# Packed expert numbers, two waits fewer per tile, and earlier offset reads and result scatters in a mixture-of-experts kernel

## What is computed

```python
x = x + tanh(g_xattn) * xattn(layernorm(x), ctx, ctx)
n = layernorm(x)
logits = n @ Wr + br
idx, gate = argmax(logits), softmax(logits)[argmax]
h = gelu(n @ W1[idx] + b1[idx])          # 128 -> 512
x = x + tanh(g_ffn) * gate * (h @ W2[idx] + b2[idx])
```

## Time and profile before

| | |
|---|---|
| three runs | 315.43, 316.87, 317.26 us; median 316.87 |
| profiled execution | 315.37 us, of which the span is 313.5 |
| mean granted clock of TensorE | 0.924 |
| busy, share of the span | PE 78%, DVE 61%, ACT 53%, POOL 58% |
| the chain that ended last | PE 42%, DVE 13%, nothing shown ("issue") 12%, POOL 10%, ACT 5%, unknown 5% |

### The profile page before, as it was taken

How to read it: one execution, slowest core, us unless ns; L and a number is a source line. 1 busy time by engine, 2 the same in 40 slices (tenths; PEclk the granted TensorE clock), 3 DMA queues, 4 the chain that set the end, 5 groups by cost and what they waited for, 6 DMA issues and landing times.

```text
span 313.5 us, 10518 instructions
## 1 busy us (share of the span) xinstructions
PE 245.5 (78%) x3529; PEld 212.7 (68%) x3529; DVE 191.3 (61%) x638; ACT 166.8 (53%) x481; POOL 182.3 (58%) x222
## 2 busy tenths in 40 slices
PE   1467899988999878889898668697457499999970
PEld 1245778777777756777686547586357499999960
DVE  5548688889898999779977745557023044444420
ACT  2155788877787866787776612526023144444420
POOL 7476557676597974889687630463734045444450
PEclk9997999999999999999999977859759699999995
DMA  7602556364636451525222133012233112100100
GB/s 215 207 17 38 150 140 192 65 171 119 163 89 171 110 137 26 136 47 141 44 43 42 45 79 83 29 41 88 72 92 96 44 34 64 57 28 30 36 19 0
DMA packets 58535, 26.63 MB, mean 85 GB/s; under 512 B 38608, under 2 KB 53989, under 8 KB 58484
## 3 DMA queue, kind: packets, MB, share of 16 engines
q1 hardware_dynamic: 55204, 20.15, 26.2%
q0 software_dynamic: 2272, 4.46, 4.3%
q10 hardware_dynamic: 1008, 1.34, 1.5%
HBM read 16.69 MB, written 5.51 MB: 71 GB/s over the span
## 4 chain that ended last, share of the span: by engine, by line
PE 42%; DVE 13%; issue 12%; POOL 10%; ACT 5%; SPq 5%; another core or an unknown queue 5%; DMA 3%; POOLq 1%; DVEq 0%; ACTq 0%
PE ps L736 12%; PE ps L779 4%; SPq L403 4%; DVE mx L1194 3%; PE ps L720 3%; PE ps L718 3%; PE ps L719 3%; PE ps L794 2%; POOL rot L531 2%; POOL rot_s L533 2%; PE ps L769 2%; PE ps L821 2%; POOL rot L537 2%; PE ps L818 2%
## 5 line engine op out<-in xcount | busy, mean ns | idle before, releaser
L552 POOL DMA_INDIRECT out<-fin,got x39 | 37.9, 972 | 46.2 <-DVE fin L1242 34.9
L504 POOL DMA_INDIRECT rows<-x_all,dest_i x32 | 33.4, 1044 | 29.5 <-DVE x_all L1051 22.3
L1194 DVE TENSOR_REDUCE mx<-ps 128x16 f16<-128x1024 f32 x32 | 39.1, 1221 | 17.3 <-PE ps L794 13.3
L736 PE MATMUL ps<-w_f,hT 128*128 x312 | 48.8, 304 | 0.0
L1242 DVE SCALAR_TENSOR_TENSOR fin<-ps,got 128x128 f32<-128x128 f32 x39 | 13.7, 350 | 55.8 <-PE ps L736 41.3
L736 PEld LDWEIGHTS ps<-w_f,hT 128*128 128x128 f32 x312 | 41.9, 209 | 0.8
L779 PE MATMUL ps<-vx,pr 128*64 128x32 f32 x1024 | 36.9, 226 | 4.4 <-DVE on L1129 2.6
L779 PEld LDWEIGHTS ps<-vx,pr 128*64 128x64 f32 x1024 | 33.5, 141 | 8.3 <-issue 3.1
L649 ACT ACTIVATE hT<-ps 128x512 f32<-128x512 f32 x39 | 23.3, 597 | 29.0 <-PE ps L720 15.5
L581 ACT ACTIVATE pr<-ps 128x1024 f32<-128x1024 f32 x32 | 32.7, 1023 | 10.9 <-PE ps L821 10.6
L821 PE MATMUL ps<-qT,kbd 128*128 128x64 f16 x512 | 35.3, 198 | 2.0 <-issue 2.0
(11 more groups left out here) (155 smaller groups left out, 607.8 us busy)
## 6 DMA issues: line engine op xcount, KB each, us to landing
kbd<-kT SPq DMA_DIRECT2D x128, 32.0 KB
got<-rows SPq DMA_DIRECT2D x39, 72.0 KB, 1.9
w_f<-in_W_rows SPq DMA_DIRECT2D x8, 256.0 KB, 3.0
w_r<-in_W_last_row SPq DMA_DIRECT2D x8, 256.0 KB, 3.4
w_f<-in_L_ffn_W SPq DMA_DIRECT2D x8, 256.0 KB
x_all<-in_x SPq DMA_DIRECT2D x3, 512.0 KB, 4.6
xt_all<-in_x_t SPq DMA_DIRECT2D x3, 512.0 KB, 4.5
ct_all<-in_ctx SPq DMA_DIRECT2D x3, 512.0 KB, 4.5
```

The lines of the kernel that those rows point to most:

```text
L504: pool.indirect_dma_start(out=rows, out_offset=bass.IndirectOffsetOnAxis(ap=dest_i[:, t:t + 1], axis=0), in_=x_all[:, t, :], in_offset=Non ...
L552: pool.indirect_dma_start(out=out_d, out_offset=bass.IndirectOffsetOnAxis(ap=got_i[:, u % GOT, R_ID:R_ID + 1], axis=0), in_=fin[:, u % FRI ...
L736: mm = pe.matmul(o, hT[:, par, c, :], w2_f[:, bass.ds(e, 1), c, :].rearrange("p o n -> p (o n)"), start=False, stop=(c == FC - 1))
L1194: dve.tensor_reduce(mx[:, t % 2, 0:H], ps_s[:, :].rearrange("p (h k) -> p h k", k=S), AX.X, ALU.max).then_inc(mx_done, 1)
```

## The change

1. The expert numbers are packed: a word holds eight of them as digits of three bits. DVE multiplies the comparisons with powers of 8 (`C_OCT`, te_q) and sums seven times eight of them into a word (te_w). The first part has 2 words, the second 4. te_c is padded to a whole number of words and filled with zeros at step 8. PE loads the words and takes a number out of its word by a shift and a mask, once per sorted tile in the code.
2. PE's wait for `f_lo` ahead of the transpose is left out from tile 6 on, and the wait for `f_gelu` ahead of the first layer altogether.
3. SP's first offset load of each part stands ahead of its waits for `g_sent` and `g_fill`.
4. `out_step`: the results of tiles 0, 1 and 2 are scattered at steps 39, 39 and 40, between the row scatters of steps 38 and 41; the others, from step 43 on, one in each step.

```diff
--- before.py
+++ after.py
@@ -43,11 +43,13 @@
 SPLIT = GROUPS[EARLY][1]
 N1 = math.ceil((SPLIT * P - NE * (P - 1)) / P)
 N2 = NS - N1
+PACK = 8
+W1N, W2N = math.ceil(N1 / PACK), math.ceil(N2 / PACK)
 F0 = SPLIT + 14
 STEPS = F0 + NS + 3
 FRING = 20
 
-C_ID, C_COS, C_SIN, C_IOTA, C_REV, C_POW, C_EPS, NCF = 0, 128, 136, 144, 184, 192, 193, 194
+C_ID, C_COS, C_SIN, C_IOTA, C_REV, C_POW, C_EPS, C_OCT, NCF = 0, 128, 136, 144, 184, 192, 193, 194, 202
 K_ID, K_TRI, K_ONE, K_EXP, K_SEL, K_BASE, NCH = 0, 128, 256, 384, 1408, 2432, 2440
 
 
@@ -69,6 +71,7 @@
     f[:, C_REV:C_REV + NE] = NE - np.arange(NE)[None, :]
     f[:, C_POW] = -0.5
     f[:, C_EPS] = EPS
+    f[:, C_OCT:C_OCT + PACK] = 8.0 ** np.arange(PACK)[None, :]
     h[:, K_ID:K_ID + P] = np.eye(P)
     h[:, K_TRI:K_TRI + P] = r[:, None] < r[None, :]
     h[:, K_ONE:K_ONE + P] = 1
@@ -207,10 +210,10 @@
         done = sb("done", [P, NE])
         room = sb("room", [P, NE - 1])
         jump = sb("jump", [P, 2, NE - 1])
-        te_c = sb("te_c", [1, NS, NE - 1])
+        te_c = sb("te_c", [1, (W1N + W2N) * PACK, NE - 1])
+        te_q = sb("te_q", [1, W1N + W2N, PACK, NE - 1])
         off_c = sb("off_c", [1, NS, NE - 1])
-        te_f = sb("te_f", [1, NS])
-        te_i = sb("te_i", [1, NS], I32)
+        te_w = sb("te_w", [1, W1N + W2N], I32)
         first = sb("first", [1, NS])
         off_f = sb("off_f", [1, 2, NS])
         off_i = sb("off_i", [1, NS], I32)
@@ -326,7 +329,7 @@
             return 16 * sum(1 for v in range(NS) if pair(v) % ring == pair(u) % ring and pair(v) <= pair(u))
 
         def out_step(u):
-            return max(F0 + 3 + u, max(SCATTER_AT) + 1 + u // 2)
+            return F0 + 5 + u // 2 if u < 3 else min(max(SCATTER_AT) - 2 + u, STEPS - 1)
 
         def used(which, u):
 
@@ -436,21 +439,25 @@
                     alone(sp, sp_passed)
                 sp.dma_start(got[:, slot, :], rows[bass.ds(offset, P), :]).then_inc(f_got[pair(t) % (GOT // 2)], 16)
 
-            def row_tiles(a, b):
+            def offsets(t, b):
+
+                return nc.values_load_multi_w_load_instructions(
+                    off_i[0:1, t:min(t + 8, b)], engines=[SP_ENGINE], min_val=0, max_val=SORTED - P,
+                    skip_runtime_bounds_check_because="a tile starts in the region of its expert or on the last blank rows")[1]
+
+            def row_tiles(a, b, offs):
 
                 for t in range(a, b):
-                    if (t - a) % 8 == 0:
-                        n = min(8, b - t)
-                        offs = nc.values_load_multi_w_load_instructions(
-                            off_i[0:1, t:t + n], engines=[SP_ENGINE], min_val=0, max_val=SORTED - P,
-                            skip_runtime_bounds_check_because="a tile starts in the region of its expert or on the last blank rows")[1]
+                    if t > a and (t - a) % 8 == 0:
+                        offs = offsets(t, b)
                     row_tile(t, t % GOT, offs[(t - a) % 8])
 
             sp.wait_ge(g_off, 1)
             alone(sp, sp_passed)
+            offs = offsets(0, N1)
             sp.wait_ge(g_sent[0], 16 * SPLIT)
             alone(sp, sp_passed)
-            row_tiles(0, N1)
+            row_tiles(0, N1, offs)
             sp.wait_ge(s_blank, 2)
             sp.wait_ge(g_endi, 1)
             alone(sp, sp_passed)
@@ -461,11 +468,12 @@
                 sp.dma_start(rows[bass.ds(ends[e], P), :], blank[:, :]).then_inc(g_fill, 16)
             sp.wait_ge(g_off, 2)
             alone(sp, sp_passed)
+            offs = offsets(N1, NS)
             sp.wait_ge(g_sent[1], 16 * (T - SPLIT))
             alone(sp, sp_passed)
             sp.wait_ge(g_fill, 16 * NE)
             alone(sp, sp_passed)
-            row_tiles(N1, NS)
+            row_tiles(N1, NS, offs)
 
 
         @block.gpsimd
@@ -678,17 +686,18 @@
                     mm = pe.matmul(ps_end, ones_h, oh[:, sum_at(g + 1), :], start=True, stop=True)
                 mm.then_inc(g_rank, 1)
 
-            experts = {}
+            experts, words = {}, {}
 
             def expert_numbers(u):
 
                 if u in (0, N1):
-                    a, b = (0, N1) if u < N1 else (N1, NS)
+                    a, b = (0, W1N) if u < N1 else (W1N, W1N + W2N)
                     pe.wait_ge(g_te, 1 if u < N1 else 2)
-                    regs = nc.values_load_multi_w_load_instructions(
-                        te_i[0:1, a:b], engines=[PE_ENGINE], min_val=0, max_val=NE - 1,
-                        skip_runtime_bounds_check_because="the number of an expert is a sum of seven comparisons, so 0 to 7")[1]
-                    experts.update({a + m: r for m, r in enumerate(regs)})
+                    words.update(enumerate(nc.values_load_multi_w_load_instructions(
+                        te_w[0:1, a:b], engines=[PE_ENGINE], min_val=0, max_val=8 ** PACK - 1,
+                        skip_runtime_bounds_check_because="eight digits of 0 to 7, each a sum of seven comparisons")[1]))
+                v = u if u < N1 else u - N1
+                experts[u] = (words[v // PACK] >> (3 * (v % PACK))) & 7
 
             def rows_transposed(u):
 
@@ -701,7 +710,8 @@
                 if u == 5:
                     pe.wait_ge(on_done, T)
                 pe.wait_ge(f_z, u + 1)
-                wait(pe, f_lo, used(t_bank, u))
+                if u < 6:
+                    wait(pe, f_lo, used(t_bank, u))
                 pe.transpose(bank[t_bank(u)][:, 0:P], z[:, u % 2, :], ident).then_inc(f_T, 1)
 
             def first_layer(u):
@@ -710,7 +720,6 @@
                 if u == 0:
                     pe.wait_ge(mx_done, T)
                 pe.wait_ge(f_lo, u + 1)
-                wait(pe, f_gelu, u - 1)
                 for c in range(FC):
                     o = bank[2 + par][:, P * c:P * c + P]
                     w_h = w1_h[:, bass.ds(e, 1), P * c:P * c + P].rearrange("p o n -> p (o n)")
@@ -1080,12 +1089,14 @@
             def tile_tables(k):
 
                 a, b = ((0, N1), (N1, NS))[k]
-                n = b - a
+                wa, wb = ((0, W1N), (W1N, W1N + W2N))[k]
+                n, nw = b - a, wb - wa
                 ts = slice(a, b)
-                then(dve.tensor_tensor(te_c[:, ts, :],
+                tc = slice(wa * PACK, wa * PACK + n)
+                then(dve.tensor_tensor(te_c[:, tc, :],
                                        cf[0:1, C_IOTA:C_IOTA + n].rearrange("p (n o) -> p n o", o=1).broadcast_to([1, n, NE - 1]),
                                        og(base[0:1, k, 1, 5:4 + NE], n), ALU.is_ge))
-                then(dve.tensor_tensor(off_c[:, ts, :], te_c[:, ts, :], og(jump[0:1, k, :], n), ALU.mult))
+                then(dve.tensor_tensor(off_c[:, ts, :], te_c[:, tc, :], og(jump[0:1, k, :], n), ALU.mult))
                 then(dve.tensor_reduce(off_f[:, 0, ts], off_c[:, ts, :], AX.X, ALU.add))
                 if k == 0:
                     dve.scalar_tensor_tensor(out=off_i[:, ts], in0=cf[0:1, C_IOTA:C_IOTA + n], scalar=float(P),
@@ -1093,8 +1104,13 @@
                 else:
                     then(dve.tensor_tensor(off_f[:, 1, ts], first[:, ts], off_f[:, 0, ts], ALU.add))
                     dve.tensor_scalar(off_i[:, ts], off_f[:, 1, ts], end_f[0:1, k, NE - 1:NE], None, ALU.min).then_inc(g_off, 1)
-                then(dve.tensor_reduce(te_f[:, ts], te_c[:, ts, :], AX.X, ALU.add))
-                dve.tensor_copy(te_i[:, ts], te_f[:, ts]).then_inc(g_te, 1)
+                then(dve.tensor_tensor(te_q[:, wa:wb, :, :],
+                                       te_c[:, wa * PACK:wb * PACK, :].rearrange("p (w j) e -> p w j e", j=PACK),
+                                       cf[0:1, C_OCT:C_OCT + PACK].rearrange("p (w j e) -> p w j e", w=1, e=1
+                                                                             ).broadcast_to([1, nw, PACK, NE - 1]), ALU.mult))
+                with nc.allow_low_precision(reason="whole numbers below 8 ** 8"):
+                    dve.tensor_reduce(te_w[:, wa:wb], te_q[:, wa:wb, :, :].rearrange("p w j e -> p w (j e)"), AX.X, ALU.add
+                                      ).then_inc(g_te, 1)
 
             def tiles_begun():
 
@@ -1221,6 +1237,7 @@
                     dve.tensor_copy(oh[:, 0, :], base_h).then_inc(s_oh0, 1)
                     dve.memset(base[:, :, :, :], 0.0).then_inc(s_oh0, 1)
                     dve.memset(started[:, :], float(N1)).then_inc(s_oh0, 1)
+                    then(dve.memset(te_c[:, :, :], 0.0))
                 if i == F0 - 4:
                     tile_counts(0)
                 if i == F0 - 3:
```

## The result

The changed kernel takes 307.45 us (median of 4 runs, 306.31 to 309.03) against 316.15 for the kernel before: ratio 0.973, 95% interval 0.967 to 0.980. The forecast was 302.4, the range 296 to 309. It is faster, by 8.7 us where 14.5 were summed; the time lies in the range, 1.6 us from its upper end, and 5 us above the forecast. The profiled executions are 306.31 and 315.37 us, their spans 304.5 and 313.5, so 9.0 us are to be found.

What follows compares the result with a forecast made beforehand. Only the last 125 us decide: PE's stop at the second load, POOL's burst, then a stage bound by PE's work per tile. Terms sum to −14.5 us from the profiled 315.37, giving 300.9, so a median of 302.4; range 296 to 309.

Steps and rivals of the forecast that it cites:

- The second load: PE's load of 26 expert numbers before tile 13's transpose: four words instead remove the gap at 241.39, −5.7 us (−4.7 at longest).
- The half clock: PE's granted clock of 0.51 for 5.2 us after that gap goes too: −2.6 us (−1.3 to −2.6).
- Fewer waits: PE's queue in the late stage: two waits fewer, some unpacking added, pace 1.994 to 1.85 a tile, −3.2 us (0 to −5).
- rival A: On PE, unpacking as two instructions of its own eats the waits' gain; pace stays 1.99, 305.6 us; chance 0.20.
- rival D: On PE, the packed number is worked out anew for each of nine uses; pace 2.84, about 328 us; chance 0.04.
- The first load: PE's load of 13 numbers ahead of the first transpose: two words finish before row z, −0.7 us, or 0.
- Three scatters moved: Three result scatters leave POOL's burst of ten for its idle time; ACT and DVE released sooner, −2.5 us (−4.8 to +3).
- Rival B: POOL's burst isn't the cause, or moved scatters only shift the wait: 304.9 us, or 307.9 with +3; chance 0.12.
- Rival C: The stall of 222 to 230 goes altogether, needing the long burst: another 5.9 us, 296.5 us; chance 0.10.
- The offset reads: SP reads offsets before waiting for scattered rows; hidden or outside the chain, 0 us, at most −0.5.
- The tables on DVE: DVE's multiplication in place of a cast and longer tables: +0.2 us for both tables (0 to +0.5).
- E: Another wait takes the second load's place, for missing rows or later numbers: 307 to 311 us, or 316; chance 0.04.

Runs made afterwards that it cites:

- e10: As e9, with the load of the second four words moved ahead of the second layer of tile 6; 304.48 us, ratio 0.964 to the kernel before.
- e7: Changed kernel with plain numbers, loaded as 13 and then in pieces of 4, 8, 8 and 6; 293.92 us, ratio 0.982 to the kernel before.
- e1: Changed kernel with its numbers unpacked again, 13 and 26 by one load each; 294.62 us, ratio 0.985 to the kernel before.
- e9: Changed kernel with PE's f_fin wait moved into the last chunk of the first layer from tile 13 on; 304.18 us, ratio 0.967 to the kernel before.
- e3: Changed kernel with PE's two waits put back, packed numbers kept; 299.50 us, ratio 1.002 to the kernel before.
- e6: The changed kernel itself, on a chip without unnamed waits; 290.87 us, ratio 0.972 to the kernel before.
- e5: The kernel before, unchanged, run once more for its trace on a chip without unnamed waits; 298.41 us.
- e11: Changed kernel without early scatters, POOL waiting for later fins so no result stands among the five row scatters; 310.00 us, ratio 0.981 to the kernel before.
- e4: Changed kernel with the result scatters' steps of the kernel before, on a chip without unnamed waits; 291.37 us, ratio 0.971 to the kernel before.
- e12: The kernel of e4 run once more, again on a chip without unnamed waits; 291.27 us, ratio 0.972 to the kernel before.
- e8: Changed kernel with SP's offset loads back behind the waits for scattered rows; 291.27 us, ratio 0.976 to the kernel before.

## Why the prediction was right, and where its sum was off

**The second load: right.** −5.7 was forecast, or −4.7 at the least. Tiles 10 to 11 took 5.40 less. Four words took 1.02 us, between the row of five offsets (0.55) and the upper bound of 1.88. Of the 3.13 us between the two second layers 1.2 are over the pace: 0.30 with nothing to do, the rest while PE's queue has no lead on the matmuls. On PE a number or word cost 0.24 to 0.29 us in every load of 4, 6, 8 or 26 behind the first but e10's, and splitting the load (e7) won nothing: the count had to fall.

**The half clock: right, mis-sized.** −2.6 (−1.3 to −2.6) was forecast, −1.52 came between tiles 11 and 12. The granted clock stayed at 1.00, but the reference pace of 1.78, from which the excess was worked out, was not to be had any more.

**Fewer waits: the step that failed in size.** The forecast had −3.2, at a pace of 1.85, for 23 tiles. Found is 0.66 less over 20 of them and 0.04 over the last three with the tail. The three tiles ahead of them took 0.45 more, so it is −0.2 in all. This is rival A. The mechanism was the right one, and the places in PE's queue count it out: 1.78 us with 14 (e1, where the matmuls bind), 1.87 with 15 (e9), 1.96 changed and 1.99 before with 16 each, 2.20 with 18 (e3). The two waits gave 0.23 (2.195 − 1.961), as forecast. The unpacking took 0.20 back (2.195 − 1.994), where 0.09 was taken: shift and mask were not folded into the register instructions of the uses but stand as two of their own. The prediction's 17 places were 16, and the nine uses in its rival D are 13, which changes nothing in the forecast.

And the three tiles that ran at 1.78 before, behind the half clock, run at 1.93 now. Before, PE's queue ran ahead while PE was slow and lived on that: line 734 has one register instruction and one matmul a tile, and the one was 1.7 us ahead of the other at 252.1 and 0.3 at 257.5.

```profile
L734 PEldq FUSED_REGOPS  x1: 60/60/60, 250.4 to 250.4; - x1
L734 PE MATMUL ps<-b_h,ch x1: 301/301/301, 252.1 to 252.1; 128*128 128x128 f16 x1
...
L734 PEldq FUSED_REGOPS  x1: 60/60/60, 257.2 to 257.2; - x1
L734 PE MATMUL ps<-b_h,ch x1: 219/219/219, 257.5 to 257.5; 128*128 128x128 f16 x1
```

In the changed kernel the lead is 0.1 to 0.2 us at 241.5, 243.4 and 249.2. So the 1.78 of those three tiles was a refund of the stop, which the sum had not seen.

**The first load: not shown.** −0.7 was forecast. The first transpose came later in this trace (195.73 for 193.99) and sooner on another chip (190.62 for 191.79). Over the nine traces from chips without unnamed waits it lies between 190.6 and 193.2, with no order by the size of the first load.

**Three scatters moved: the gain came, and a late start took half of it.** −2.5 net, with +3 as the cost if they hold others; 1.78 is what tiles up to 6 won, first load and all. The prediction's long burst is three shorter, and the moved ones have a wait of 2.96 us behind them. What they cost the last group is less than the later start of its scatters: of the 2.5 us, 2.0 were there at the pair of row scatters ahead of the first moved result, and nothing shows where they come from (1.7 of them stood at the first transpose). From that pair to the last group's scatters it is 9.28 us for 8.78, so 0.5; on the chips without unnamed waits 6.45 for 6.11 (e6, e5); in e11, which moves nothing, 8.19. From the pair to the second layer of tile 6 it is 20.55 us for 24.35, 3.8 less. These are single traces.

That a row of indirect DMAs holds up ACT and DVE on such a chip is shown by e11, by its place and by its release: it moved with the rows of scatters, and the wait ends 2.07, 1.68 and 1.13 us after the burst's last member, with bursts of 10, 7 and 5, and 0.74 after three. What in a burst does it, the issuing or the transfers, no run tells. Rival B (the burst isn't the cause) is out with that. Rival C (the stall needs the long burst) is out: ACT stood 4.16 us there even with five. What moving the three is worth by itself there stays open; on other chips it is nothing (e4, e6, e12).

**The offset reads: right.** 0 forecast, 0.4 us within the noise (e8). The tables on DVE: nothing in the chain shows them.

**The other side.** D, an unpacking at each use, did not happen: two more instructions a tile. E's wait in the load's place neither; PE went on at 240 with tile 13's rows there.

**The sum.** Forecast against found: −5.7 and −5.4; −2.6 and −1.5; −3.2 and −0.2; −0.7 and −2.5 together against −1.8. More than half of the 5.5 us that were missing is the pace. Every gain came out smaller than forecast, so the time ended beyond rival A's 305.6, and the width of the range and not the middle of it carried the forecast. Of the signs that were named, a second layer every 1.8 to 1.9 us did not come (1.96), the third of the moved results went out at 216.15 and not by 214, and the loads took 0.73 and 1.02 us for about 0.5; that the gap is gone, the burst of seven and ACT's longest wait (6.2 for 7) came.

## What to carry to other kernels

When PE is full and each tile takes longer than its matmuls alone, count what stands between them in its queue: here every wait with a place of its own, though other waits covered it, and every register instruction cost about 0.12 us, and above 14 of them the pace was their number. A wait that a register instruction could carry cost nothing (e9). Price what replaces a wait in the same coin before counting the wait as won. A stop also lends time to what follows it, so its removal here was worth 0.45 us less than its length and its aftermath. And a transfer order that seems free on one chip may be paid for on another: look at both traces before moving it.

## What the runs showed of the hardware

A load of numbers into PE's registers took 0.24 to 0.29 us a number when it was 4, 6, 8 or 26 of them behind the first load, but 0.12 in e10 (0.46 us for four at 230.4). The first 13 took 0.10 each (1.30 us in every trace that has them), the first two words 0.36 each. SP read eight offsets in 0.30 to 1.95 us. So the count alone does not give the price, and what else does is open.

The same kernel took 316 us on some chips and 299 on others. Most of the difference lies in unnamed waits of ACT and DVE at and behind rows of indirect DMAs on POOL, up to 11.2 us long: they have 5% of the chain of the kernel before in its first trace, some 16 us of 313.5, and none of it in e5, whose span is 16.9 us shorter. On e11's chip they come with three of them 1.27 us apart and not with single ones; in the traces of e1 to e8 and e12 there are none even with sixteen in a row (e5). Why the chips differ, no run here tells.
